# A macaron transformer layer on one core: in the last group of heads GpSimd adds the exponentials of four key tiles before the product with ones

## The chip, the cores and the metric

The kernel runs on 1 core of one Trainium2 chip. The metric is the device time of one execution in microseconds (us). Before the change it is 2382.53 us, the median of three runs (2381.05 to 2382.56).

Engines are called TensorE (PE in the rows; PEld is its weight load), VectorE (DVE), ScalarE (ACT), GpSimd (POOL) and SyncE (SP, which issues the DMAs).

## The reference

For each of 8 sequences of 1024 tokens and 512 features the layer computes a routed half step, an attention step and a second routed half step:

```
x = x + 0.5 * ffn(layernorm(x))
x = x + attention(layernorm(x))
x = x + 0.5 * ffn(layernorm(x))

ffn(x):        scores = x @ w_router
               the 3/4 of the tokens with the highest scores become gelu(x @ w_block), the others stay
attention(x):  Q = x @ Wq.T, per head times q_to_latent; latent keys and values of 64 features
               logits = q_lat . latent_k / 8, causal; attn = softmax(logits)
               heads = (attn @ latent_v) @ v_up; out = heads @ Wout.T
```

There are 16 heads of 32 features. What the change touches is the denominator of the softmax: for each query, the sum of the exponentials over all keys.

## The kernel before

**Tiles.** The 8 sequences are called batches 0 to 7 here. The 1024 tokens are 8 tiles of 128 (keys) and 2 blocks of 512 (queries). The 16 heads are 4 groups of 4 heads. All products run in float32 in three passes of high and low parts, except those with the exponentials.

**The order.** One function, `program_order`, writes a single list of events for all engines. Each engine walks that list and issues its own part of each event, in the list's order; semaphores hold it back where it needs another engine. Event names are tuples such as `("DEN", b, g, c, j)`: batch, group of heads, query block, key tile.

**Attention.** A group of heads takes 9 units (`SCORES`), called units 0 to 8 below. Units 0 to 3 are query block 1 against the full key tiles 0 to 3, 512 queries wide; units 4 to 6 are the diagonal tiles 4 to 7 of block 1 (and a piece of block 0), units 7 and 8 are block 0. In each unit:

- `S`: TensorE computes the scores of the 4 heads into 4 PSUM banks (lines 842 and 845, four passes), and ScalarE writes their exponentials into one of four slots `pr`, 128 partitions x 4 heads x 512 (line 809, four instructions).
- `AM`: GpSimd zeroes the triangle of a diagonal tile (line 715).
- `PV` and `DEN`, two units later: TensorE multiplies the exponentials by the values (line 950), and by a block of ones (line 957) to get the denominators. `PV` and `DEN` gather in one bank each over the key tiles of a query block; `LAST_TILE` says which tile is last. `HT`, `HR`, `HE` on VectorE turn, invert and multiply (lines 1116, 1119, 1121, 1127).
- A slot of `pr` is used again four units later, and ScalarE waits there for the `DEN` that read it.

**PSUM.** The units take banks from a queue of six. In the last group, `S` of units 1 to 3 waits for all four exponentials of the unit before. `S` of units 4 to 8 takes three banks of the unit before, freed by its first three exponentials, and one more: that of `SC` for unit 4, and for units 5, 6 and 7 that of the transposes `T` of unit 3, 4 and 5, which VectorE frees when it has written the low part (line 1018).

**What else runs in the last group.** In groups 0 to 2 each unit also holds products for the row maxima of the next group (`MX`, line 856) and VectorE reduces them. The last group, number 3, has none. In batches 0 to 6 it holds the first steps of the next batch instead, in this order of the list:

- `T` and `NO`, one tile per unit: ScalarE normalises (line 744), TensorE transposes (line 871), ScalarE copies the high part (line 723), VectorE subtracts it (line 1018).
- `SD`, 8 instructions in units 0 and 1: VectorE multiplies a token tile by the router's weights and sums it (line 1028, two operands from SBUF). `SM` turns four of these sums into scores (line 1035, two operands from SBUF, 4 columns). The first `SM` stands in unit 0, the second in unit 1.
- `SC`: TensorE spreads the scores over the partitions (line 877). The first `SC` stands ahead of `S` of unit 2, the second ahead of `S` of unit 3.
- `RT` for tile 0 to 7, two per unit in units 3 to 6: VectorE counts how many scores are higher (lines 1043, 1045, and 1047, which reads two operands from SBUF). In the list, `T`'s subtraction of unit 4 stands behind `RT` of tiles 0 and 1.
- `RF` and then `GX` on GpSimd (line 702, 8 instructions), in unit 7, and the first two tiles of the next batch's `F` (line 829).

In batch 7 there is no next batch. The last group holds copies of finished heads there: `HS`, a copy on ScalarE (line 723) and a subtraction on GpSimd (line 709, 128x512, two operands from SBUF).

Of the kernel before, what the change touches and what calls it, by code (L numbers as in the profile page):

```python
# [9 lines left out]
ALU = mybir.AluOpType  # L10
# [32 lines left out]

def diagonal(c, j):
    return j >= TC * c
# [12 lines left out]
ADDED = [[(1, 0)], [(1, 1)], [(1, 2)], [(1, 3)], [(1, 4)], [(1, 5), (1, 7)], [(1, 6)], [(0, 0), (0, 2)], [(0, 1), (0, 3)]]  # L58
UNITS = len(SCORES)
# [40 lines left out]
def program_order():  # L100
# [89 lines left out]
    def attention(b):  # L190
# [15 lines left out]
        def mask(n):  # L206
            g, u = units[n]
            return [("AM", b, g, c, j) for c, j in SCORES[u] if diagonal(c, j)]

        def added(n, add):  # L210
            g, u = units[n]
            return [(add, b, g, c, j) for c, j in ADDED[u]]

# [124 lines left out]
def macaron(nc, x, w_q, w_lat, w_qk, w_vu, w_out, w_router, w_block, scratch_q, scratch_o, spill_x, out):  # L338
# [47 lines left out]
    for e in sched:  # L386
# [48 lines left out]
        if k in ("PV", "DEN") and e[4] > 0:  # L435
            continue
# [6 lines left out]
    with ExitStack() as ctx:  # L443
# [14 lines left out]
        def sem(name):  # L458
            return ctx.enter_context(nc.semaphore(name))
# [16 lines left out]
        prs = [over(f"pr{n}", region[n], [P, SLOTS, HQ, BANK]) for n in range(3)]  # L476
        raw_b, raw_o, raw_q = (over(f"raw_{w}", region[0] + 8192 * n, [P, NK, E]) for n, w in enumerate("boq"))
# [54 lines left out]
        s_done, exp_ready, mask_ready = sem("s_done"), sem("exp_ready"), sem("mask_ready")  # L532
        pv_done, ac_ready, den_done, den_free = sem("pv_done"), sem("ac_ready"), sem("den_done"), sem("den_free")
# [40 lines left out]
        def pr_of(b, g, u):  # L574
            return prs[(b + 2) % 3][:, (0, 2, 1, 3)[step_nth[b, g, u] % SLOTS], :, :]

# [96 lines left out]
        def _(eng):  # L673
# [16 lines left out]
            for e in sched:  # L690
# [13 lines left out]
                elif k == "HS":  # L704
# [5 lines left out]
                                            ).then_inc(hsl_ready, 1)  # L710
                elif k == "AM":
# [7 lines left out]
        def _(eng):  # L719
# [9 lines left out]
            for e in sched:  # L729
# [68 lines left out]
                elif k == "S":  # L798
# [3 lines left out]
                    if n >= SLOTS:  # L802
                        was = steps[n - SLOTS]
                        act.wait_ge(den_done, max(nth["DEN", *was[0:2], *seg] for seg in SCORES[was[2]]))
# [14 lines left out]
        def _(eng):  # L819
# [42 lines left out]
            for e in sched:  # L862
# [90 lines left out]
                elif k == "DEN":  # L953
                    b, g, c, j = e[1:]
                    own, w = exps_of(b, g, c, j)
                    for h in range(HQ):
                        m = eng.matmul(bank(e)[h * DH:(h + 1) * DH, BANK - w:BANK], ones[:], own[:, h, :],  # L957
                                       start=(j == 0), stop=(j == LAST_TILE[c]), skip_group_check=True)
# [9 lines left out]
        def _(eng):  # L968
# [17 lines left out]
            for e in sched:  # L986
# [124 lines left out]
                elif k == "HT":  # L1111
# [4 lines left out]
                    nc.vector.transpose(rden[:], bank(("DEN", b, g, c, 0))).then_inc(den_free, 1)  # L1116
# [46 lines left out]
```

## Time and profile before

| | us |
|---|---|
| median of three runs | 2382.53 |
| the profiled execution, whole | 2386.42 |
| its span, first to last instruction | 2384.7 |
| TensorE busy | 2201.2 (92%) |
| VectorE busy | 1805.1 (76%) |
| ScalarE busy | 1176.3 (49%) |
| GpSimd busy | 404.6 (17%) |

The span is what the rows add up to; the whole execution holds 1.7 us around it. Busy time of TensorE counts overlapping instructions once. A timeline row begins with its start and its length in us, counted from the start of the span; where several instructions are merged (xN), the start is that of the first and the length that of all. The eight batches repeat every 287 to 291 us.

### The profile page before, as it was taken

How to read it: one execution, taken by the hardware profiler on the slowest of the kernel's cores; microseconds unless marked ns; L12 is line 12 of the kernel's file. 1: busy time of each engine (PE TensorE's matmuls, PEld its weight loads, DVE VectorE, ACT ScalarE, POOL GpSimd, SP SyncE). 2: the span in 40 equal slices, each digit the busy share in tenths (PEclk: the TensorE clock that was granted, in tenths of full speed). 3: DMA queues.
4: the chain of work that ended last, by engine and by line, in shares of the span. 5: the costliest groups of instructions: out<-in, count | busy, mean ns of one | idle time of the engine just before them, and what ended most of it. 6: DMA issues, size and time to landing. Idle time of an engine off the chain costs nothing.

```text
span 2384.7 us, 53143 instructions
## 1 busy us (share of the span) xinstructions
PE 2201.2 (92%) x21504; PEld 1338.9 (56%) x21504; DVE 1805.1 (76%) x5077; ACT 1176.3 (49%) x2070; POOL 404.6 (17%) x510
## 2 busy tenths in 40 slices
PE   5789999999999999999998999989998999999997
PEld 4544477445674456744566446754466544765455
DVE  7668767887669877788777886788767888678747
ACT  4245643556435564345644565345643557435552
POOL 2001111212102121021210212111111111121131
PEclk9889999999999999999999999999999999999999
DMA  3200021200302002020020201211021110212000
GB/s 137 106 2 2 2 83 60 72 2 2 106 36 72 3 19 89 37 72 3 19 89 36 73 2 40 68 54 55 2 71 36 70 40 2 71 36 72 2 2 36
DMA packets 69633, 106.42 MB, mean 45 GB/s; under 512 B 2576, under 2 KB 32784, under 8 KB 67344
## 3 DMA queue, kind: packets, MB, share of 16 engines
q1 hardware_dynamic: 69392, 103.03, 12.6%
q8 instruction: 173, 2.83, 0.5%
q14 instruction: 68, 0.56, 0.1%
HBM read 64.75 MB, written 37.75 MB: 43 GB/s over the span
## 4 chain that ended last, share of the span: by engine, by line
PE 75%; DVE 13%; ACT 6%; issue 5%; POOL 1%; DMA 0%; DVEq 0%; POOLq 0%; ACTq 0%
PE psum L829 29%; PE psum L842 17%; PE psum L950 10%; PE psum L957 9%; PE psum L845 5%; ACT pr L809 3%; DVE part L1093 3%; PE psum L871 2%; PE psum L856 2%; DVE psum L1095 2%; DVE junk L1043 1%; DVE nt_l L1018 1%; DVE junk L1028 1%; DVE junk L1045 1%; ACT nt_h L723 1%
## 5 line engine op out<-in xcount | busy, mean ns | idle before, releaser
L809 ACT ACTIVATE pr<-psum 128x512 f32<-128x512 f32 x1152 | 617.7, 597 | 537.8 <-PE psum L845 537.7
L842 PE MATMUL psum<-qk,qk 32*128 32x512 f32 (+3 forms) x4608 | 516.7, 371 | 63.6 <-DVE part L1093 26.9
L1095 DVE CUSTOM_DVE_ANT_0 psum<-psum,mask_b 128x512 f32<-128x512 f32 (+3 forms) x1024 | 473.1, 522 | 106.1 <-PE psum L856 104.7
L842 PEld LDWEIGHTS psum<-qk,qk 32*128 32x128 f32 x4608 | 318.6, 187 | 386.3 <-ACT pr L809 313.9
L856 PE MATMUL psum<-qk,qk 32*128 32x512 f32 (+3 forms) x4608 | 513.1, 371 | 20.6 <-DVE part L1093 19.1
L1093 DVE TENSOR_REDUCE part<-psum 128x1 f32<-128x512 f32 x512 | 325.4, 682 | 58.5 <-PE psum L856 56.5
L856 PEld LDWEIGHTS psum<-qk,qk 32*128 32x128 f32 x4608 | 312.0, 187 | 45.5 <-DVE part L1093 22.8
L950 PE MATMUL psum<-pr,v_sb 128*32 128x512 f32 (+3 forms) x3072 | 314.3, 504 | 1.6 <-ACT ht L723 1.6
L957 PE MATMUL psum<-pr,ones 128*32 128x512 f32 (+3 forms) x3072 | 308.8, 496 | 0.0
L715 POOL TENSOR_SCALAR_AFFINE_SELECT pr<-pr 128x512 f32<-128x512 f32 x256 | 161.6, 650 | 835.2 <-ACT pr L809 835.2
L744 ACT ACTIVATE norm<-x,nmr,rstd 128x512 f32<-128x512 f32 x192 | 153.3, 816 | 163.0 <-DVE nmr L1012 163.0
L845 PE MATMUL psum<-mrow,minus 1*128 1x512 f32 (+3 forms) x1536 | 217.4, 348 | 0.0
L829 PE MATMUL psum<-wb_h,nt_h 128*128 128x512 f32 x512 | 207.7, 406 | 3.0 <-ACT nt_act L768 3.0
L829 PE MATMUL psum<-wb_h,nt_l 128*128 128x512 f32 x512 | 200.9, 392 | 0.0
L1018 DVE TENSOR_TENSOR nt_l<-psum,nt_h 128x512 fp32r<-128x512 f32 x192 | 130.5, 684 | 93.0 <-ACT nt_h L723 92.6
L829 PE MATMUL psum<-wb_l,nt_h 128*128 128x512 f32 x512 | 200.8, 392 | 0.0
L702 POOL TENSOR_SCALAR x<-x,gain,shift 128x512 f32<-128x512 f32 x128 | 110.5, 879 | 358.3 <-DVE gain L1060 358.3
L871 PE MATMUL psum<-ident,norm 128*128 128x128 f32 x768 | 122.4, 289 | 30.7 <-ACT norm L744 22.8
L723 ACT ACTIVATE qk<-psum 128x512 fp32r<-128x512 f32 x128 | 76.2, 596 | 147.1 <-PE psum L829 146.9
L723 ACT ACTIVATE nt_h<-psum 128x512 fp32r<-128x512 f32 x192 | 115.9, 606 | 58.9 <-PE psum L871 58.8
L1095 DVE DVE_READ_ACCUMULATOR2_ANT part<- 128x1 f32 x1024 | 144.7, 141 | 0.0
L999 DVE BATCH_NORM_STATS2 stats<-x 128x6 f32<-128x512 f32 x192 | 131.9, 690 | 10.8 <-DMA x<-x_dram 6.5
(109 smaller groups left out, 3239.1 us busy)
## 6 DMA issues: line engine op xcount, KB each, us to landing
x<-x_dram SPq DMA_DIRECT2D x16, 1024.0 KB, 7.1
spill_x<-x SPq DMA_DIRECT2D x16, 1024.0 KB, 4.8
x<-spill_x SPq DMA_DIRECT2D x16, 1024.0 KB, 7.2
out_dram<-x SPq DMA_DIRECT2D x14, 1024.0 KB, 5.1
w_h<-scratch_o SPq DMA_DIRECT2D x28, 256.0 KB, 3.1
w_l<-scratch_o SPq DMA_DIRECT2D x28, 256.0 KB, 3.3
w_h<-scratch_q SPq DMA_DIRECT2D x6, 1024.0 KB, 4.9
w_l<-scratch_q SPq DMA_DIRECT2D x6, 1024.0 KB, 6.9
```

Of the source, the lines that this page charges most:

```text
L715: nc.gpsimd.affine_select(out=tri, in_=tri, compare_op=ALU.is_ge, fill=0.0, base=0, pattern=[[0, HQ], [1, P]], channel_multiplier=-1).then ...
L723: return nc.scalar.activation(dst, src, ACT.Copy)
L809: nc.scalar.activation(pr_of(b, g, u)[:, 2 * p + place, :], bank(e, place), ACT.Exp, scale=SCALE).then_inc(exp_ready, 1)
L829: m = eng.matmul(o, a_cols(lhs, k), b_cols(rhs, k), start=(k == 0 and t == 0), stop=(k == n - 1 and t == 2))
L842: eng.matmul(o, (k_h, k_h, k_l)[t][own, P * j:P * (j + 1)], (q_h, q_l, q_h)[t][own, queries], start=(t == 0 and at == 0), stop=False, skip ...
L845: m = eng.matmul(o, minus[row_at:row_at + 1, :].broadcast_to([1, P]), mrow[row_at:row_at + 1, queries], start=False, stop=True, skip_group ...
L856: m = eng.matmul(bank(e, place)[:, at:at + w], (q_h, q_h, q_l)[t][own, P * i:P * (i + 1)], (k_h, k_l, k_h)[t][own, BANK * block:BANK * blo ...
L871: m = eng.transpose(bank(e)[:, n * P:(n + 1) * P], norm[:, slot, n * P:(n + 1) * P], ident[:])
L950: m = eng.matmul(bank(e)[h * DH:(h + 1) * DH, BANK - w:BANK], v_sb[:, j, P * g + DH * h:P * g + DH * (h + 1)], own[:, h, :], start=(j == 0 ...
L957: m = eng.matmul(bank(e)[h * DH:(h + 1) * DH, BANK - w:BANK], ones[:], own[:, h, :], start=(j == 0), stop=(j == LAST_TILE[c]), skip_group_ ...
L1093: m = nc.vector.tensor_reduce(top_of, scores, AX_X, ALU.max)
L1095: m = nc.vector.tensor_tensor_reduce(scores, scores, mask_b[:, BANK - w:BANK], 1.0, FAR, ALU.add, ALU.max, top_of)
```

## The change

For query block 1 of the last group, GpSimd adds the exponentials of key tiles 0 to 3 into a buffer `acc` (event `AD`, three additions of 128x2048 elements per batch), and the product with ones runs once on that sum in place of four times. `DEN` of key tiles 0, 1 and 2 is gone in that group; `DEN` of key tile 3 reads `acc` and begins the sum. `acc` lies where the queries and keys of group 2 were. A slot of units 0 to 3 is now given back by `PV` and `AD` and no more by `DEN`.

```diff
+def first_tile(e):
+
+    return ADDENDS - 1 if e[0] == "DEN" and e[2] in SUMMED and e[3] == 1 else 0
...
+SUMMED, ADDENDS = (NQ - 1,), 4
...
         def mask(n):
             g, u = units[n]
+            if g in SUMMED and 0 < u < ADDENDS:
+                return [("AD", b, g, u)]
             return [("AM", b, g, c, j) for c, j in SCORES[u] if diagonal(c, j)]
 
         def added(n, add):
             g, u = units[n]
+            if add == "DEN" and g in SUMMED and u < ADDENDS - 1:
+                return []
             return [(add, b, g, c, j) for c, j in ADDED[u]]
...
+        accs = [[over(f"acc{n}_{m}", region[n] + 16384 * m, [P, HQ, BANK]) for m in range(2)] for n in range(3)]
...
+        def acc_of(b, g):
+
+            return accs[(b + (g - 1) // 2) % 3][(g - 1) % 2]
...
+                elif k == "AD":
+                    b, g, j = e[1:]
+                    pool.wait_ge(exp_ready, 2 * nth["S", b, g, j, 1])
+                    if j > 1:
+                        pool.wait_ge(add_ready, nth[e] - 1)
+                    acc = acc_of(b, g)
+                    nc.gpsimd.tensor_tensor(acc[:], exps_of(b, g, 1, 0)[0] if j == 1 else acc[:], exps_of(b, g, 1, j)[0], ALU.add
+                                            ).then_inc(add_ready, 1)
...
                     if n >= SLOTS:
                         was = steps[n - SLOTS]
-                        act.wait_ge(den_done, max(nth["DEN", *was[0:2], *seg] for seg in SCORES[was[2]]))
+                        if was[1] in SUMMED and was[2] < ADDENDS:
+                            act.wait_ge(pv_done, nth["PV", *was[0:2], 1, was[2]])
+                            act.wait_ge(add_ready, nth["AD", *was[0:2], max(was[2], 1)])
+                        else:
+                            act.wait_ge(den_done, max(nth["DEN", *was[0:2], *seg] for seg in SCORES[was[2]]))
...
                 elif k == "DEN":
                     b, g, c, j = e[1:]
                     own, w = exps_of(b, g, c, j)
+                    if c == 1 and g in SUMMED and j == ADDENDS - 1:
+                        own = acc_of(b, g)
+                        pe.wait_ge(add_ready, nth["AD", b, g, j])
                     for h in range(HQ):
                         m = eng.matmul(bank(e)[h * DH:(h + 1) * DH, BANK - w:BANK], ones[:], own[:, h, :],
-                                       start=(j == 0), stop=(j == LAST_TILE[c]), skip_group_check=True)
+                                       start=(j == first_tile(e)), stop=(j == LAST_TILE[c]), skip_group_check=True)
                     m.then_inc(den_done, 1)
```

What the list makes of it, on the two engines concerned. On TensorE, in the last group of batch 2, units 2 and 3 before (L842 and L845 are the scores, L950 `PV`, L871 the transposes, L957 `DEN`, L877 `SC`):

```order
L845 MATMUL psum<-mrow,minus 128x512 x4
L950 MATMUL psum<-pr_93,v_sb 32x512 x4
L871 MATMUL psum<-ident,norm 128x128 x4
L957 MATMUL psum<-pr_93,ones 32x512 x4
L877 MATMUL psum<-ident,scol 128x128 x4
L842 MATMUL psum<-qk_4_63,qk_6_65 128x512 x4
```

and now, where the same lines are numbered 874, 979, 900, 906 and 871:

```order
L874 MATMUL psum<-mrow,minus 128x512 x4
L979 MATMUL psum<-pr_93,v_sb 32x512 x4
L900 MATMUL psum<-ident,norm 128x128 x4
L906 MATMUL psum<-ident,scol 128x128 x4
L871 MATMUL psum<-qk_4_63,qk_6_65 128x512 x4
```

The `DEN` between the transposes and `SC` is gone, and likewise in units 3 and 4; in unit 5 it stands where it stood.

On GpSimd, the last two groups of batch 2 before (L715 `AM`, L702 `GX`):

```order
L715 AFFINE_SELECT pr_93<-pr_93 128x4x128 x15
L702 TENSOR_SCALAR x_49<-x_49,gain,shift 128x512 x8
L715 AFFINE_SELECT pr_93<-pr_93 128x4x128 x3
```

and now, with `AD` as line 734 and lines 715 and 702 as 740 and 719:

```order
L740 AFFINE_SELECT pr_93<-pr_93 128x4x128 x10
L734 TENSOR_TENSOR acc_0_95<-pr_93 128x2048
L734 TENSOR_TENSOR acc_0_95<-acc_0_95,pr_93 128x2048 x2
L740 AFFINE_SELECT pr_93<-pr_93 128x4x128 x5
L719 TENSOR_SCALAR x_49<-x_49,gain,shift 128x512 x8
L740 AFFINE_SELECT pr_93<-pr_93 128x4x128 x3
```

Three additions stand ahead of the group's first `AM`. In batch 7 `HS` stands between the second addition and the third:

```order
L734 TENSOR_TENSOR acc_0_99<-pr_92 128x2048
L734 TENSOR_TENSOR acc_0_99<-acc_0_99,pr_92 128x2048
L726 TENSOR_TENSOR nt_l<-ht,nt_h 128x4x128
L734 TENSOR_TENSOR acc_0_99<-acc_0_99,pr_92 128x2048
L726 TENSOR_TENSOR nt_l<-ht,nt_h 128x4x128
L740 AFFINE_SELECT pr_92<-pr_92 128x4x128
```

No instruction of VectorE or SyncE is added, removed or moved.

## Rows read from the trace of the kernel before

**Rows 1.** The page: busy time of the engines, and the chain's shares.
```profile
PE 2201.2 (92%) x21504; PEld 1338.9 (56%) x21504; DVE 1805.1 (76%) x5077; ACT 1176.3 (49%) x2070; POOL 404.6 (17%) x510
PE 75%; DVE 13%; ACT 6%; issue 5%; POOL 1%; DMA 0%; DVEq 0%; POOLq 0%; ACTq 0%
```
**Rows 2.** Groups of instructions by form: busy us, mean ns of one, idle before them.
```profile
L957 PE MATMUL psum<-pr,ones 128*32 128x512 f32 x1536 | 205.6, 607 | 0.0
...
L709 POOL TENSOR_TENSOR nt_l<-ht,nt_h 128x512 fp32r<-128x512 f32 x64 | 82.2, 1288 | 248.4 <-ACT nt_h L723 248.4
```
**Rows 3.** Timeline of TensorE, batch 3's last group, second SC and units 3 to 6.
```profile
1137.61 0.98 PE L842 MATMUL psum<-qk,qk 32*128 32x512 f32 x12
...
1141.79 0.62 PE L877 MATMUL psum<-ident,scol 128*128 128x128 f32 x4 [0.40 <-DVE scol L1035]
1142.34 0.97 PE L842 MATMUL psum<-qk,qk 32*128 32x512 f32 x12
...
1145.06 1.06 PE L957 MATMUL psum<-pr,ones 128*32 128x512 f32 x8
1146.05 0.97 PE L842 MATMUL psum<-qk,qk 32*128 32x512 f32 x12
...
1149.76 1.08 PE L842 MATMUL psum<-qk,qk 32*128 32x384 f32 x24
...
1153.63 0.98 PE L842 MATMUL psum<-qk,qk 32*128 32x256 f32 x24
```
**Rows 4.** Timeline of ScalarE, the same group: exponentials of units 1 to 3.
```profile
1134.15 2.07 ACT L809 ACTIVATE pr<-psum 128x512 f32<-128x512 f32 x4 [1.38 <-PE psum L845]
...
1138.84 2.07 ACT L809 ACTIVATE pr<-psum 128x512 f32<-128x512 f32 x4 [0.47 <-PE psum L845]
...
1143.59 2.07 ACT L809 ACTIVATE pr<-psum 128x512 f32<-128x512 f32 x4 [0.54 <-PE psum L845]
1145.51 0.63 ACT L723 ACTIVATE nt_h<-psum 128x512 fp32r<-128x512 f32 x1
1145.99 0.84 ACT L744 ACTIVATE norm<-x,nmr,rstd 128x512 f32<-128x512 f32 x1
```
**Rows 5.** Timeline of VectorE, the same group.
```profile
1135.95 0.75 DVE L1028 SCALAR_TENSOR_TENSOR junk<-x,mv,wr 128x512 bf16<-128x512 f32 x1
...
1136.74 0.16 DVE L1035 TENSOR_TENSOR scol<-dots,rstd 128x4 f32<-128x4 f32 x1
...
1141.48 0.16 DVE L1035 TENSOR_TENSOR scol<-dots,rstd 128x4 f32<-128x4 f32 x1
...
1150.13 0.68 DVE L1018 TENSOR_TENSOR nt_l<-psum,nt_h 128x512 fp32r<-128x512 f32 x1
```
**Rows 6.** Timelines of GpSimd and VectorE where both read SBUF; the last pair is a counter-case.
```profile
2.84 0.29 POOL L687 TENSOR_SCALAR_AFFINE_SELECT earlier<-earlier 128x128 bf16<-128x128 bf16 x1
...
1169.86 1.81 POOL L715 TENSOR_SCALAR_AFFINE_SELECT pr<-pr 128x512 f32<-128x512 f32 x3
...
1169.97 2.24 DVE L1066 SCALAR_TENSOR_TENSOR x<-nt_act,sel,x 128x512 f32<-128x512 f32 x1 [2.74 <-ACT nt_act L768]
...
1270.95 1.01 POOL L697 TENSOR_TENSOR rstd<-var,half 128x4 f32<-128x4 f32 x1 [12.10 <-DVE var L1007]
...
1271.38 0.74 DVE L1028 SCALAR_TENSOR_TENSOR junk<-x,mv,wr 128x512 bf16<-128x512 f32 x1
```
**Rows 7.** Stretches of batch 3's first group: TensorE's busy time, granted clock; a `PV` there.
```profile
1011.30:1014.70 3.40, 1.62 (x28) 1.02 (x24) 3.36 (x13) 2.85 (x4) 0.00 (x0) 1.00 0.00 0
1014.70:1018.10 3.40, 1.74 (x20) 1.15 (x16) 3.40 (x9) 1.08 (x2) 0.00 (x0) 0.50 0.00 0
...
1018.87 1.94 PE L950 MATMUL psum<-pr,v_sb 128*32 128x512 f32 x8
```
**Rows 8.** Batch 7's last group: exponentials of unit 1, `DEN` of key tile 3.
```profile
2289.55 2.06 ACT L809 ACTIVATE pr<-psum 128x512 f32<-128x512 f32 x4 [2.13 <-PE psum L845]
...
2302.48 1.04 PE L957 MATMUL psum<-pr,ones 128*32 128x512 f32 x8
```

More of the change, by code:

```diff
@@ L434, in macaron @@
             continue
-        if k in ("PV", "DEN") and e[4] > 0:
+        if k in ("PV", "DEN") and e[4] > first_tile(e):
             continue
@@ L532, in macaron @@
         s_done, exp_ready, mask_ready = sem("s_done"), sem("exp_ready"), sem("mask_ready")
+        add_ready = sem("add_ready")
         pv_done, ac_ready, den_done, den_free = sem("pv_done"), sem("ac_ready"), sem("den_done"), sem("den_free")
@@ L1115, in _ @@
                         dve.wait_ge(heads_ready, nth[e] - 1)
-                    nc.vector.transpose(rden[:], bank(("DEN", b, g, c, 0))).then_inc(den_free, 1)
+                    nc.vector.transpose(rden[:], bank(("DEN", b, g, c, LAST_TILE[c]))).then_inc(den_free, 1)
                 elif k == "HR":
```

## The prediction

> **What bounds the kernel now.** I read the page first. TensorE is busy 92% of the span and holds 75% of the chain that ended last; VectorE holds 13% [rows 1]. So a product taken off TensorE is worth something, unless another engine is just behind it at that place. GpSimd is busy 17%, the lowest of all, which makes it look free. Then I read the last group of heads engine by engine, in batch 3; the start of that group looks alike in batches 0 to 6. On TensorE it is a chain of short steps, and two of them wait: the second `SC` waited 0.40 for VectorE's second `SM` [rows 3]. VectorE's two `SM` start at 1136.74 and 1141.48, and `SC` starts 0.15 after the second has ended (1141.64 to 1141.79) [rows 3, 5]. ScalarE starts a unit's exponentials 1.2 after the scores start (1137.61 to 1138.84) and needs 1.92 for four of them, 0.48 for the high part behind them and about 0.7 for a normalisation [rows 3, 4]. So in this group VectorE's small router steps lie between TensorE's products, and the question is what GpSimd's additions do to VectorE.
>
> **What is removed.** Three `DEN` in each of 8 batches, 24 in all. One takes TensorE 0.99 (1145.06 to the next scores at 1146.05) [rows 3]; the group's mean of 607 ns is that of instructions that overlap in fours [rows 2]. At most 24 x 0.99 = 23.8 us go. But `DEN` of unit 2 stood ahead of the `SC` that waits for `SM`: its 0.99 buys nothing. Behind units 3 and 4 the scores need the first three exponentials of the unit before, and ScalarE's own round is 1.92 + 0.48 + 0.7 = 3.1 against the present 3.7 (1142.34 to 1146.05) [rows 3, 4]. So two rounds shrink by 0.6, and a part of the rest comes back later: S of unit 6 could stand some 1.4 earlier. Undisturbed the removal is worth 1.4 a batch, not 3.
>
> **What is added.** 24 additions of 128x2048 on GpSimd. No row has that size. The nearest has the same operation on a quarter of it: 1.29 [rows 2]. From above, four of them: 5.2. From below, the part that does not grow is taken off three times: 128x128 took 0.29 and 128x512 takes 1.81/3 = 0.60 in another operation [rows 6], so 0.19 is fixed, and 4 x 1.10 + 0.19 = 4.6. I take 4.6, since one instruction pays its fixed part once. The Trainium skill (GPSIMD Engine Reference, section Performance versus the Vector engine) states 4497 ns for this size; by it each figure below would shrink by 0.1.
>
> **Where it collides.** `CB` on VectorE, which reads two operands from SBUF, was ready at 1169.97 and ended at 1172.21, 0.54 after GpSimd's three selects ended at 1171.67; it should take 0.75, as its like in rows 5 does [rows 5, 6]. So it stood still while GpSimd ran. `SD`, `SM`, `RT`'s last instruction and `HE` are of that kind; `T`'s subtraction, with one operand in PSUM, isn't. Against this stands one pair: an `SD` at 1271.38 took its normal 0.74 beside a GpSimd instruction of 1.01 [rows 6]. That one reads only 4 columns, so it may have read them before; an addition of 2048 columns reads nearly to its end. The Trainium skill (SBUF — State Buffer, section Who interferes with whom) says that such a VectorE instruction and a GpSimd instruction that reads SBUF exclude each other, whoever is first, for the whole instruction. The rows show it for 0.6 us pieces and speak against the word "whole" in the case of 4 columns; by the rule an addition blocks for its full length, by the counter-case for its reading part.
>
> **The sum for batches 0 to 6**, in batch 3's times, each with the shift from before.
> 1. The first addition may start when unit 1's exponentials end, 1134.15 + 2.07 = 1136.22 [rows 4]. VectorE is in an `SD` until 1136.70; the first `SM` comes at 1136.74 [rows 5]. GpSimd is already waiting, so it goes first, until about 1136.65 + 4.6 = 1141.25. `SM`, `SC` and the scores of unit 2 follow: `SC` at 1141.5, scores at 1142.05 in place of 1137.61. Shift +4.4.
> 2. TensorE has stood for nearly 5 us. In the first group a stretch of 3.4 us with 1.62 busy was followed by one at a granted clock of 0.50, that is 1.2 GHz, in which a `PV` took 1.94 [rows 7], where a product of the same size takes 1.06 in the last group [rows 3]. At that level `SC` and the scores of unit 2 take 1.2 more. The exponentials of unit 2 start at 1144.5, not 1138.84, and end at 1146.6.
> 3. VectorE's second `SM` comes at most 4.74 after the first, as before [rows 5], and a little less, since the high part it had to wait for is there by now: 1145.7 to 1146.0. The second addition asks at 1146.6, too late to block it. The scores of unit 3 follow the exponentials, at 1146.75: shift +4.4.
> 4. Units 3 and 4 run at ScalarE's pace, with `DEN` gone: exponentials of unit 3 from 1148.2, scores of unit 4 at 1149.8 (+3.7), those of unit 5 at 1152.95 (+3.2). Here the removal pays 1.2.
> 5. The second addition runs from 1146.7 to 1151.3 and holds up `HE`; the third starts once `HE` is through, 1151.9 to 1156.5. `RT` of tile 0 reaches its two-operand instruction at about 1153.6 and waits until 1156.5. Behind it stands `T`'s subtraction of unit 4, which frees a bank for the scores of unit 6. It starts about 1.8 later, 1158.3, and ends at 1158.9. Before it started at 1150.13 [rows 5]. The scores of unit 6 stand at 1158.95 instead of 1153.63 [rows 3]: +5.3.
> 6. The last `AM`, `GX` and `CB` come some 3 us later relative to TensorE; TensorE has six more `F` to do before the first transposes that need them, and that work covers it; without it the 3 us would be added. Net +5.4, and 7 x 5.4 = 38.
>
> **Batch 7** has no router work, but GpSimd's queue has `HS` among the additions. The third ends 3 x 4.6 + 1.3 = 15.1 after 2291.61, at 2306.7; `DEN` of key tile 3 stood at 2302.48 [rows 8], so TensorE loses 4.2 there, less nothing, since every other unit follows `DEN` in the queue. With a spell at the low clock: 5. The `AM`s behind it are late but their `PV`s are too.
>
> Sum: +43 on the profiled execution's 2386.42 us gives 2429. That execution is 3.9 above the median of 2382.53, so I predict 2425. Edits that cost nothing: the two new waits of ScalarE on `AD` (unit 5 needs only the first addition, over by 1141.3; unit 7 the third, over by 1156.5, before even the scores of unit 6), and the bank that `DEN` opens with, free long before.
>
> **The rivals.**
> A, *no exclusion*: GpSimd and VectorE run side by side, as the counter-case allows. Then batches 0 to 6 gain 1.4 each and batch 7 still loses 5 to its queue: -10 + 5, 2377. For it: one pair in rows 6, and an addition that reads two operands in turn may leave gaps. Against: `CB` stood still over three instructions. This is the case that ends on the other side; it decides if `SM` ends within 0.5 of its old place behind the `SD`.
> B, *both `SM` blocked*: if the clock stays high, step 2's exponentials end at 1145.4 and the second addition takes the port at the end of the last `SD`, before the second `SM` (1145.7). `SC` then comes at 1150.2, and the third addition still hits `RT`. The same walk gives +7.5 a batch: 7 x 7.5 + 5 = 57, 2440. The third addition passing `HE` in step 5 costs the same.
> C, *only the first wait matters*: step 5's wait for the bank is covered. Then +3.3 a batch and 28 in all: 2410.
> That the additions don't replace the products is excluded by the order of instructions.
>
> **How the numbers follow.** Forecast 0.57, A 0.11, B 0.17, C 0.15. With 5.2 in place of 4.6 for an addition, steps 1, 3 and 5 add some 1.2 a batch, 9 in all. The range takes C with its lower edge, the forecast and B up to that term: 2403 to 2447; A is left out, with a little at either end. No change means within 0.2%, 4.8 us, about what a measurement of this kernel can tell. A falls just at that edge and is split, 0.06 faster and 0.05 same. All others are slower: 0.89.
>
> **What would show it.** Right: additions of 4.6; the first `SM` of batches 0 to 6 lasting some 4.6 instead of 0.16, and TensorE waiting over 4 us ahead of the first `SC`; seven spells at clock 0.50 behind it; the second `SM` short; one of `RT`'s two-operand instructions lasting about 3; scores of unit 6 waiting for VectorE. Wrong: all `SM` at 0.16 (A), two long ones per batch (B), or additions above 5.2 or below 4.3.

## The result, and the profile after

The changed kernel takes 2427.45 us (median of 4 runs, 2425.38 to 2431.34) against 2382.55 (4 runs) of the kernel before beside it: ratio 1.0191, 95% interval 1.0177 to 1.0205. It is slower by 45 us; the forecast was 2425.0 in a range of 2403 to 2447. The profiled execution took 2428.03, its span is 2426.0 at a mean granted clock of 0.967 (before: 2386.42, 2384.7 and 0.975).

The page of the changed kernel: busy time, and shares of the chain that ended last, as in [rows 1].

```profile
PE 2194.8 (90%) x21312; PEld 1342.7 (55%) x21312; DVE 1872.6 (77%) x5077; ACT 1175.6 (48%) x2070; POOL 521.9 (22%) x534
PE 68%; DVE 18%; ACT 7%; issue 5%; POOL 1%; DMA 0%; DVEq 0%; POOLq 0%; ACTq 0%
```

TensorE issues 192 matmuls less and is less busy, yet the span is 41 longer. What grew on the chain is VectorE, 13% to 18%, although VectorE has no instruction more. The groups of instructions of the changed kernel say which of its instructions became longer.

```profile
L1159 DVE TENSOR_TENSOR ht<-ht,rden 128x512 f32<-128x512 f32 x64 | 66.6, 1041 | 3.0 <-DVE rden L1153 0.5
L1079 DVE SCALAR_TENSOR_TENSOR junk<-srow,scol,earlier 128x128 bf16<-128x128 f32 x128 | 62.0, 484 | 0.0
L1067 DVE TENSOR_TENSOR scol<-dots,rstd 128x4 f32<-128x4 f32 x32 | 34.4, 1074 | 1.1
...
L734 POOL TENSOR_TENSOR acc<-acc,pr 128x2048 f32<-128x2048 f32 x16 | 74.8, 4676 | 38.8 <-ACT pr L838 38.1
L734 POOL TENSOR_TENSOR acc<-pr 128x2048 f32<-128x2048 f32 x8 | 37.9, 4741 | 54.3 <-ACT pr L838 54.3
```

These are `HE`, the last instruction of `RT`, and `SM`: the three kinds that read two operands from SBUF while an addition runs (L734). Their means before were 0.69, 0.37 and 0.16 us. An addition has a mean of 4.68 to 4.74 us.

Batch 3's last group on VectorE and GpSimd (start, duration, idle before it in brackets). The group begins 12.54 later than before, by the exponentials of units 0 and 1.

```profile
1148.49 0.75 DVE L1060 SCALAR_TENSOR_TENSOR junk<-x,mv,wr 128x512 bf16<-128x512 f32 x1
...
1149.29 4.33 DVE L1067 TENSOR_TENSOR scol<-dots,rstd 128x4 f32<-128x4 f32 x1
...
1157.78 0.16 DVE L1067 TENSOR_TENSOR scol<-dots,rstd 128x4 f32<-128x4 f32 x1
...
1161.04 3.10 DVE L1159 TENSOR_TENSOR ht<-ht,rden 128x512 f32<-128x512 f32 x1
1164.20 0.69 DVE L1050 TENSOR_TENSOR nt_l<-psum,nt_h 128x512 fp32r<-128x512 f32 x1
1164.81 1.27 DVE L1077 TENSOR_SCALAR_CACHE_REDUCE junk<-srow,scol 128x1024 bf16<-128x1024 f32 x1
...
1166.00 2.73 DVE L1079 SCALAR_TENSOR_TENSOR junk<-srow,scol,earlier 128x128 bf16<-128x128 f32 x1
...
1170.72 0.68 DVE L1050 TENSOR_TENSOR nt_l<-psum,nt_h 128x512 fp32r<-128x512 f32 x1
```

```profile
1148.84 4.76 POOL L734 TENSOR_TENSOR acc<-pr 128x2048 f32<-128x2048 f32 x1 [6.86 <-ACT pr L838]
1159.04 4.55 POOL L734 TENSOR_TENSOR acc<-acc,pr 128x2048 f32<-128x2048 f32 x1 [5.44 <-ACT pr L838]
1163.75 4.83 POOL L734 TENSOR_TENSOR acc<-acc,pr 128x2048 f32<-128x2048 f32 x1 [0.16 <-ACT pr L838]
```

The reader is to lay the two side by side. The first `SM` begins 0.45 after the first addition and ends at 1153.62, 0.02 after it (1153.60). `HE` ends 0.55 after the second (1163.59 to 1164.14), nearly its own 0.69. `RT`'s instruction with two operands ends 0.15 after the third (1168.58 to 1168.73). Between them, with the third addition under way, `T`'s subtraction (one operand in PSUM) takes its 0.69 and a comparison over 1024 columns with one SBUF operand its 1.27. So the number of SBUF operands decides here, not the size. (One instruction in another run does not fit; it stands in the last section.)

TensorE in the same stretch, and below it the stretch of the wait and the two behind it (columns: busy PE, PEld, DVE, ACT, POOL with their counts, then granted clock).

```profile
1153.77 1.08 PE L906 MATMUL psum<-ident,scol 128*128 128x128 f32 x4 [4.52 <-DVE scol L1067]
...
1160.37 0.98 PE L871 MATMUL psum<-qk,qk 32*128 32x512 f32 x12
...
1171.45 0.98 PE L871 MATMUL psum<-qk,qk 32*128 32x256 f32 x24 [1.04 <-DVE nt_l L1050]
```

```profile
1149.40:1153.70 4.30, 0.00 (x0) 0.00 (x0) 4.30 (x2) 1.03 (x2) 4.20 (x1) 0.95 0.00 0
1153.80:1157.20 3.40, 3.40 (x24) 2.02 (x28) 3.33 (x9) 0.90 (x2) 0.00 (x0) 0.50 0.02 5
1157.30:1160.70 3.40, 3.40 (x20) 1.84 (x16) 1.75 (x6) 2.56 (x6) 1.66 (x1) 0.59 0.00 0
```

TensorE does nothing for 4.3 us and then works at a granted clock of 0.50, 1.2 GHz. The first `SM` takes 4.33 or 4.34 and the first `SC` waits 4.52 or 4.53 in each of batches 0 to 6. **A measure for all runs:** the stretch from the exponentials of unit 1 to those of unit 8 in a last group, less the same stretch before. It says how much later the group ends than it would have, had it run as before. In batches 0 to 6 of the change it is +5.34, +5.36, +4.99, +5.65, +5.37, +5.42 and +6.27, in batch 7 +6.63, together 45.0. The exponentials of the very last unit come 42.9 late; the other 2.1 were won and lost outside these groups. No run was made on those 2 us, so their cause is not shown.

Batch 7 on TensorE and GpSimd:

```profile
2343.37 1.94 PE L989 MATMUL psum<-acc,ones 128*32 128x512 f32 x8 [4.56 <-POOL acc L734]
```

```profile
2332.70 4.83 POOL L734 TENSOR_TENSOR acc<-acc,pr 128x2048 f32<-128x2048 f32 x1
2337.49 1.27 POOL L726 TENSOR_TENSOR nt_l<-ht,nt_h 128x512 fp32r<-128x512 f32 x1
2338.73 4.49 POOL L734 TENSOR_TENSOR acc<-acc,pr 128x2048 f32<-128x2048 f32 x1
```

There the sum itself is late. The units follow each other every 3.0 us in this group and an addition takes 4.5 to 4.8, so the product waits 4.56 for the third, which stands behind an `HS` in GpSimd's queue.

### The profile page after: what moved, and what is told of

Read it like the earlier page. It is cut to its first block, busy times and chain, and to the rows that moved or that the text cites. A ratio compares the mean times of both kernels' runs of the same rounds, so it can differ in the third digit from the quotient of the medians.

```text
span 2426.0 us, 52807 instructions
## 1 busy us (share of the span) xinstructions
PE 2194.8 (90%) x21312; PEld 1342.7 (55%) x21312; DVE 1872.6 (77%) x5077; ACT 1175.6 (48%) x2070; POOL 521.9 (22%) x534
## 4 chain that ended last, share of the span: by engine, by line
PE 68%; DVE 18%; ACT 7%; issue 5%; POOL 1%; DMA 0%; DVEq 0%; POOLq 0%; ACTq 0%
PE psum L858 28%; PE psum L871 15%; PE psum L979 9%; PE psum L989 7%; PE psum L874 4%; ACT pr L838 4%; DVE part L1125 3%; DVE junk L1077 2%; PE psum L885 2%; DVE junk L1075 2%; DVE psum L1127 2%; DVE nt_l L1050 2%; DVE junk L1079 2%; PE psum L900 1%; DVE scol L1067 1%
## 5 line engine op out<-in xcount | busy, mean ns | idle before, releaser
L871 PE MATMUL psum<-qk,qk 32*128 32x512 f32 (+3 forms) x4608 | 522.7, 376 | 76.2 <-ACT pr L838 30.4
L871 PEld LDWEIGHTS psum<-qk,qk 32*128 32x128 f32 x4608 | 322.7, 190 | 393.7 <-ACT pr L838 312.2
L979 PE MATMUL psum<-pr,v_sb 128*32 128x512 f32 (+3 forms) x3072 | 320.9, 514 | 2.9 <-ACT ht L748 1.6
L989 PE MATMUL psum<-pr,ones 128*32 128x512 f32 (+3 forms) x2816 | 273.3, 485 | 0.0
L714 POOL TENSOR_TENSOR rstd<-var,half 128x4 f32<-128x4 f32 x48 | 48.6, 1012 | 510.1 <-DVE var L1039 510.0
```

The source lines that it names most:

```text
L871: eng.matmul(o, (k_h, k_h, k_l)[t][own, P * j:P * (j + 1)], (q_h, q_l, q_h)[t][own, queries], start=(t == 0 and at == 0), stop=False, skip ...
```

## The experiments

The theory to test: a two-SBUF-operand instruction of VectorE waits for the addition under way, and TensorE waits for it; the removal is worth 1.4 a batch. The rivals: the loss is the removal's or the clock's own; GpSimd's queue makes it; any work on GpSimd does. Each ratio is to runs of the kernel before that were made beside the run. "b0-6" is the mean over seven batches of the measure above, "b7" that of the last batch, both from ScalarE's timelines of the profiled execution.

| run | us | ratio to before, interval | b0-6 | b7 |
|---|---|---|---|---|
| the change | 2427.45 | 1.0191 (1.0177 to 1.0205) | +5.49 | +6.63 |
| additions_alone | 2429.04 | 1.0192 (1.0178 to 1.0206) | +5.80 | +5.55 |
| removal_alone | 2374.40 | 0.9958 (0.9945 to 0.9970) | -1.34 | -0.13 |
| split_additions | 2426.78 | 1.0187 (1.0173 to 1.0201) | +5.00 | +7.41 |
| scalar_product | 2463.18 | 1.0325 (1.0304 to 1.0346) | +8.60 | +5.95 |
| dots_early | 2399.99 | 1.0071 (1.0058 to 1.0084) | +0.24 | +7.00 |
| dots_early_before | 2380.93 | 0.9995 (0.9986 to 1.0004) | -0.84 | 0.00 |
| one_input | 2397.85 | 1.0069 (1.0051 to 1.0086) | +2.37 | -0.09 |
| groups_1_2 | 2413.97 | 1.0131 (1.0117 to 1.0144) | -0.02 | -0.01 |
| late_sum | 2440.22 | 1.0240 (1.0226 to 1.0254) | +6.71 | +6.55 |
| two_additions | 2375.00 | 0.9970 (0.9958 to 0.9981) | -1.98 | +0.73 |
| later_comparisons | 2375.96 | 0.9975 (0.9965 to 0.9986) | -2.64 | +7.61 |
| best | 2370.76 | 0.9947 (0.9933 to 0.9960) | -2.65 | 0.00 |

**additions_alone: the additions without the removal.**

```diff
...
-            if add == "DEN" and g in SUMMED and u < ADDENDS - 1:
-                return []
...
-                    if c == 1 and g in SUMMED and j == ADDENDS - 1:
-                        own = acc_of(b, g)
-                        pe.wait_ge(add_ready, nth["AD", b, g, j])
```

ScalarE waits for `DEN` and for `AD` before it uses a slot again.

> The additions run as in the change, but nobody uses their sums: TensorE does all of the DEN products as before. Theory (the additions block VectorE, the removal is worth 1.4 us a batch): the stalls of the change stay (first SM some 4.3 us in each of 7 batches, the SC of the first half waits 4.5 us), and the 8 x 1.4 = 11 us that the removal paid are lost: 2435 to 2440 us. Rival (part of the loss comes from the removal itself, by leaving TensorE without work that would keep its clock up while it waits): 2420 to 2427, since the three DEN products fall into the gaps; the DEN of unit 0 stands behind the stalled SC, so this rival is weak for the first stall.

Measured: 2429.0, within 2 us of the change. The first `SM` and the first `SC` wait as before the edit (rows of VectorE and TensorE, batch 3):

```profile
1154.13 4.33 DVE L1060 TENSOR_TENSOR scol<-dots,rstd 128x4 f32<-128x4 f32 x1
```

```profile
1158.61 1.09 PE L902 MATMUL psum<-ident,scol 128*128 128x128 f32 x4 [4.52 <-DVE scol L1060]
```

The additions cost 5.8 us a batch though nobody uses them: the loss is theirs. But the 11 us that I expected on top of 2427 did not come. In the change the removal pays 0.3 a batch (5.80 against 5.49), not 1.4. Batch 7 loses 5.55 here, although no product waits for the sum. TensorE stands for a mask there, which GpSimd has behind its additions:

```profile
2345.05 1.93 PE L975 MATMUL psum<-pr,v_sb 128*32 128x512 f32 x8 [4.16 <-POOL pr L738]
```

**removal_alone: the removal without the additions.** The mask list returns nothing in place of `AD`, and the first `DEN` reads tile 3 alone, so the denominators lack key tiles 0 to 2. The run is there for its time only.

```diff
...
-                return [("AD", b, g, u)]
+                return []
...
```

> No additions; TensorE leaves out the DEN products of the key tiles 0 to 2 in the last group, so the denominators of the second block lack these tiles there. Theory: the gain of the removal with nothing against it is 1.4 us in each of 8 batches, 2371 us (2368 to 2374), not 3 x 0.99 x 8 = 24 us (2359), because TensorE waits at SC for SM in any case. Rival (the products only fill waits): 2382, same as before. The first SM is 0.16 us again.

Measured: 0.42% faster, 8.7 us; -1.32 to -1.35 in each of batches 0 to 6. In batch 7 nearly nothing (-0.13), where the expectation had counted a full share: there the units follow each other every 3.0 us with and without `DEN`. So the removal's worth in a batch was sized right, and it is real only where nothing else holds unit 6 up. Both runs together name what does: in the change TensorE waits 1.04 before unit 6 for `T`'s subtraction behind the held `RT` (row above); what units 3 to 5 won is given back there.

**split_additions: four pieces of 128x512.**

```diff
-                    acc = acc_of(b, g)
-                    nc.gpsimd.tensor_tensor(acc[:], exps_of(b, g, 1, 0)[0] if j == 1 else acc[:], exps_of(b, g, 1, j)[0], ALU.add
-                                            ).then_inc(add_ready, 1)
+                    acc, was, own = acc_of(b, g), exps_of(b, g, 1, 0)[0], exps_of(b, g, 1, j)[0]
+                    for h in range(HQ):
+                        m = nc.gpsimd.tensor_tensor(acc[:, h, :], was[:, h, :] if j == 1 else acc[:, h, :], own[:, h, :], ALU.add)
+                    m.then_inc(add_ready, 1)
```

> Each addition of 128x2048 is issued as four of 128x512 (some 1.2 us each). Theory (a VectorE operation with two SBUF inputs waits until the GpSimd instruction under way has ended, then goes first): the first SM takes at most 1.3 us in place of 4.33, HE and the comparison with equality at most 1.9 and 1.6; the first SC waits at most 1.5 us more than before; 2427 falls to 2385 to 2400 us. Rival 1 (GpSimd keeps the port over instructions that follow at once): SM stays at 4.3 us and the time at 2427 or above, since four instructions have more fixed cost. Rival 2 (clock phases make most of the loss): 2410 to 2420.

The time was missed (2426.8 against 2385 to 2400), the mechanism held. VectorE and GpSimd in batch 3:

```profile
1152.33 1.10 DVE L1068 TENSOR_TENSOR scol<-dots,rstd 128x4 f32<-128x4 f32 x1
...
1153.95 1.24 DVE L1061 SCALAR_TENSOR_TENSOR junk<-x,mv,wr 128x512 bf16<-128x512 f32 x1
...
1155.23 1.65 DVE L1061 SCALAR_TENSOR_TENSOR junk<-x,mv,wr 128x512 bf16<-128x512 f32 x1
...
1158.60 1.62 DVE L1061 SCALAR_TENSOR_TENSOR junk<-x,mv,wr 128x512 bf16<-128x512 f32 x1
...
1160.26 1.10 DVE L1068 TENSOR_TENSOR scol<-dots,rstd 128x4 f32<-128x4 f32 x1
```

```profile
1151.88 6.12 POOL L735 TENSOR_TENSOR acc<-pr 128x512 f32<-128x512 f32 x4 [6.87 <-ACT pr L839]
1158.15 5.66 POOL L735 TENSOR_TENSOR acc<-acc,pr 128x512 f32<-128x512 f32 x4
```

VectorE does get in between two pieces: no wait is longer than one piece. But now each `SD` of the second half waits 0.4 to 0.9 too, both `SM` take 1.10, and it is the second `SC` that waits 4.60 and more, while the first waits 1.30. In the change the one long wait of `SM` had kept the `SD`s behind it clear of the addition: all 128 `SD` took 0.71 to 0.75 there. I had counted the waits that I saw, not those that they were shielding.

**scalar_product: `SM` no longer held.** Four products of one column, each with a per-partition scalar.

```diff
-                    nc.vector.tensor_tensor(scol[:, own], dots[:, own], rstd[:, 2 * f, own], ALU.mult).then_inc(scol_ready, 1)
+                    for i in range(TC * c, TC * (c + 1)):
+                        m = nc.vector.tensor_scalar(scol[:, i:i + 1], dots[:, i:i + 1], rstd[:, 2 * f, i:i + 1], None, ALU.mult)
+                    m.then_inc(scol_ready, 1)
```

> The SM of four columns, one tensor_tensor product of two SBUF tiles, is issued as four tensor_scalar products of one column each with a per-partition scalar; all else as in the change. Theory (only operations that stream two SBUF inputs are held off): the four take some 0.5 us together though the addition is under way, the first SC waits under 1 us, and what is left is the wait of HE and of the comparison with equality behind the later additions, and batch 7: 2393 us (2385 to 2402). Rival 1 (any VectorE read of SBUF after a GpSimd start waits, or SM waits for a semaphore of the addition): SM's first column takes 4.3 us, 2427. Rival 2 (HE and RT would cost as much once SM does not wait): 2415 to 2425.

The worst run of all, 1.0325. Batch 3 on VectorE, GpSimd and TensorE:

```profile
1170.32 0.58 DVE L1068 TENSOR_SCALAR scol<-dots,rstd 128x1 f32<-128x1 f32 x4
...
1171.41 3.82 DVE L1060 SCALAR_TENSOR_TENSOR junk<-x,mv,wr 128x512 bf16<-128x512 f32 x1
...
1175.27 4.86 DVE L1060 SCALAR_TENSOR_TENSOR junk<-x,mv,wr 128x512 bf16<-128x512 f32 x1
```

```profile
1169.88 4.81 POOL L734 TENSOR_TENSOR acc<-pr 128x2048 f32<-128x2048 f32 x1 [6.87 <-ACT pr L838]
1174.98 4.61 POOL L734 TENSOR_TENSOR acc<-acc,pr 128x2048 f32<-128x2048 f32 x1 [0.30 <-ACT pr L838]
```

```profile
1182.97 1.08 PE L906 MATMUL psum<-ident,scol 128*128 128x128 f32 x4 [8.59 <-DVE scol L1068]
```

`SM` passes the addition (0.58 for four), as the theory has it. It waits for the same semaphores as before, so none of them was what held it. The wait moves to the two `SD` behind it: the first is held by addition one, the second by addition two, which is ready at once because TensorE was not held up. The second `SC` then waits 8.59. This is rival B of the prediction with other victims.

**dots_early, and its control dots_early_before.** The same edit in the change and in the kernel before.

```diff
-                chunks[i // 2] += dot(0, b + 1, i)
+                groups[2][8 + i] += dot(0, b + 1, i)
```

> The change with the eight dot products of the next batch's router and their two SM moved from the first eight halves of the last group into the group before it, where GpSimd adds nothing. Theory: the 4.5 us wait of the first SC and the clock that falls after it are gone in 7 batches; HE and the first comparison with equality still wait behind the second and third addition (up to 3 us each), which delays the T subtraction of unit 4 by some 2 us, of which the removal pays 1.3: 0 to +1.5 us a batch; batch 7 keeps its 6.6: 2380 to 2400 us, 2390 likeliest. Rival (HE and the comparison are worth as much as SM): 2415 to 2427.

> The kernel before with the same move of the dot products. Theory: VectorE has the room for 6 us more in the group before the last (70% busy there), the 0.4 us wait of SC goes: 2376 to 2384 us. Rival (VectorE is short of time beside the maxima and holds TensorE up): 2390 or more; then the cost belongs to the move and is taken off the reading of dots_early.

The control is equal to before (0.9995): it loses 0.94 a batch in the third group and wins 0.84 in the last. With nothing of two operands before `SC`, the change falls from 2427 to 2400: 27 us of its 45 went with the `SM` wait and its clock. Of the 18 that are left, 7.0 is batch 7 and 6.5 is the third group, which is longer by what the control shows. In the last groups of batches 0 to 6 only step 5 of the prediction remains (VectorE, then TensorE, batch 3):

```profile
1144.24 4.51 DVE L1159 TENSOR_TENSOR ht<-ht,rden 128x512 f32<-128x512 f32 x1
...
1150.47 2.85 DVE L1079 SCALAR_TENSOR_TENSOR junk<-srow,scol,earlier 128x128 bf16<-128x128 f32 x1
```

```profile
1155.80 0.98 PE L871 MATMUL psum<-qk,qk 32*128 32x256 f32 x24 [1.42 <-DVE nt_l L1050]
```

By the exponentials of batch 3, counted from unit 1, unit 5 stands 2.85 earlier than before and unit 6 only 0.44: the held `RT` takes 2.4 back, which `HE`, held for 4.51, does not. In batches 0 and 5 a spell at the low clock follows that wait, and the group ends 1.0 late; in the other five it ends 0.05 to 0.11 early.

**one_input: GpSimd reads one operand.** It writes one tile's exponentials over `acc` in place of adding, so the denominators lack key tiles 0 to 2.

```diff
-                    acc = acc_of(b, g)
-                    nc.gpsimd.tensor_tensor(acc[:], exps_of(b, g, 1, 0)[0] if j == 1 else acc[:], exps_of(b, g, 1, j)[0], ALU.add
+                    nc.gpsimd.tensor_scalar(acc_of(b, g)[:], exps_of(b, g, 1, j)[0], 1.0, 0.0, ALU.mult, ALU.add
                                             ).then_inc(add_ready, 1)
```

> In place of each addition GpSimd writes the unit's exponentials times 1 plus 0 (tensor_scalar, one SBUF input, 128x2048), so the denominators lack the key tiles 0 to 2 in the last group. By the GX of 128x512 at 0.91 us each takes 3.6 to 3.7 us. Theory (a GpSimd instruction that streams SBUF holds VectorE's two-input reads off, whatever its own number of inputs; GX and CB stand so in the kernel before): the first SM takes 3.3 us, the time falls by about 7 x 1 for the shorter instruction: 2408 to 2422 us. Rival (only a GpSimd instruction of two inputs holds it off): SM 0.16 us, 2371 to 2380 us.

```profile
1142.96 2.15 POOL L733 TENSOR_SCALAR acc<-pr 128x2048 f32<-128x2048 f32 x1 [6.87 <-ACT pr L837]
```

```profile
1143.40 1.72 DVE L1066 TENSOR_TENSOR scol<-dots,rstd 128x4 f32<-128x4 f32 x1
```

The size was wrong: an instruction has 1.98 us in the mean, not 3.6, and the time lies below the expected range. The mechanism held: `SM` begins inside it and ends 0.01 after it (1145.11 to 1145.12). So it isn't GpSimd's number of operands that holds VectorE; a shorter instruction costs less, 16 us in all against 45. The mean of +2.37 hides a spread from +0.24 to +4.07: in batches 1, 2, 3, 5 and 6 GpSimd's second instruction comes just ahead of the second `SM`, holds it for 1.8 as well, and TensorE waits 2.64 to 2.66 for the second `SC`. In batches 0 and 4 it comes after it.

**groups_1_2: the sums in the second and third group.**

```diff
-SUMMED, ADDENDS = (NQ - 1,), 4
+SUMMED, ADDENDS = (1, 2), 4
```

> The sums are made in the second and third group of heads and not in the last. VectorE's operations there read PSUM and at most one SBUF tensor (maxima, statistics); only HE reads two. Theory: the three DEN products of 0.99 us that go in each group shorten it where TensorE is the bound (96% busy there), HE waits up to 4.3 us behind the first addition and delays the maxima queued behind it: between -2.5 and +2.5 us a group, 16 groups: 2343 to 2423 us, 2375 likeliest. Rival (the additions cost about 5 us wherever they stand, because GpSimd slows VectorE's every read of SBUF): 2445 or more.

Measured 1.0131, inside the wide expected range, but by another way. The third group takes as long as before to 0.1 us: three `DEN` gone and nothing gained; what sets that group's length was not tested. The second loses 5.2 in batch 3 (37.4 in all). VectorE and GpSimd there:

```profile
1078.52 2.32 DVE L1039 TENSOR_SCALAR var<-mv 128x4 f32<-128x4 f32 x1
...
1086.50 0.16 DVE L1044 SCALAR_TENSOR_TENSOR nmr<-mv,rstd 128x4 f32<-128x4 f32 x1 [2.29 <-POOL rstd L714]
```

```profile
1075.89 9.60 POOL L734 TENSOR_TENSOR acc<-acc,pr 128x2048 f32<-128x2048 f32 x2
1085.43 1.04 POOL L714 TENSOR_TENSOR rstd<-var,half 128x4 f32<-128x4 f32 x1
```

The statistics of the next batch pass through both engines: `VA` is held, then `RS` stands behind the additions in GpSimd's queue, then `NM` waits 2.29 for it, with the maxima behind `NM`. `HE`, which I had named, slipped through between two additions. Batch 7 has the additions too, but no next batch whose statistics could be held, and its second group loses 0.04.

**late_sum: the sum used two units later.**

```diff
-            if add == "DEN" and g in SUMMED and u < ADDENDS - 1:
+            if add == "DEN" and g in SUMMED and u < ADDENDS:
                 return []
-            return [(add, b, g, c, j) for c, j in ADDED[u]]
+            late = [(add, b, g, 1, ADDENDS - 1)] if add == "DEN" and g in SUMMED and u == ADDENDS + 1 else []
+            return [(add, b, g, c, j) for c, j in ADDED[u]] + late
...
```

> The change, but TensorE takes the product with the sum two units later (after the DEN products of unit 5) and starts the accumulation with the DEN of unit 4. Theory: in batches 0 to 6 the sum was there in time and nothing changes (+5.4 us each stays); in batch 7 the 4.56 us wait for the third addition goes, and with it most of the 6.6 us: 2427.5 - 5.5 = 2422 us (2418 to 2425). Rival (the wait moves in batch 7 to the exponentials or to HE): 2427. Rival (the early wait for the sum costs in every batch): 2410 or less.

The forecast was missed: the run is slower than the change. Batch 7 keeps +6.55; TensorE, then GpSimd:

```profile
2353.51 1.94 PE L980 MATMUL psum<-pr,v_sb 128*32 128x512 f32 x8 [4.25 <-POOL pr L741]
```

```profile
2352.83 0.62 POOL L741 TENSOR_SCALAR_AFFINE_SELECT pr<-pr 128x512 f32<-128x512 f32 x1
```

`DEN` no longer waits, and the `PV` of unit 4 does, for the mask `AM` that stands behind the same additions and two `HS`. Batch 7's price is GpSimd's queue, whoever waits for it, as additions_alone had shown; the expectation's first rival was right in kind. In the other batches the moved product makes it 1.2 a batch dearer: TensorE waits for `T` before unit 6 in any case (1.54 to 2.67 here, at most 1.42 in the change), and a product that had filled this wait stands where none is.

**two_additions.** dots_early and late_sum together, with `ADDENDS` 3.

```diff
-SUMMED, ADDENDS = (NQ - 1,), 4
+SUMMED, ADDENDS = (NQ - 1,), 3
```

> Three key tiles summed by two additions in place of four by three (ADDENDS 3), the dot products early as in dots_early, the sum used two units later. Theory: nothing two-input of VectorE that TensorE waits for meets an addition any more (HE does, with 2 us of slack behind it), so the 2.4 us that the T subtraction of unit 4 gave back in dots_early stay: about -2.2 + 0.9 = -1.3 us a batch, batch 7 within 1 us of before: 2372 us (2368 to 2378), below both kernels. Rival (HE behind the second addition holds the T subtraction of unit 3 long enough to stop TensorE): 2380 to 2390.

0.30% faster than before, 6.8 us. Without the third addition `RT` isn't held (0.35 at most), and the 2.4 us stay (-1.98 within the last group, +0.9 in the one before). The forecast of 2372 was 3 too low, in the range.

**later_comparisons.** dots_early and late_sum, three additions, and

```diff
-                chunks[6 + i] += [("RT", 0, b + 1, i)]
+                chunks[8 + i] += [("RT", 0, b + 1, i)]
...
-            chunks[14] += [("RF", 0, b + 1)]
+            chunks[16] += [("RF", 0, b + 1)]
```

> All three additions, the dot products early, the sum used two units later, and the eight comparisons RT one unit later (8 + i in place of 6 + i), so that the T subtraction of unit 4 stands ahead of the one that the third addition holds. Theory: the 2.85 us won by unit 5 stay, less 0.9 in the group before: -1.9 us a batch, batch 7 +1 to +2: 2370 us (2366 to 2378). Rival (the comparisons then end too late for GX and the next projection): what is won is lost at the first F of the next batch, 2382 or more.

-2.64 a batch, 0.7 better than two_additions: with `T`'s subtraction ahead of the held comparison the third addition costs nothing. The comparisons end in time. Batch 7 was mis-sized, +7.6 and not +1 to +2, by the queue that additions_alone and late_sum show.

**best.** later_comparisons with the last batch as before:

```diff
-            if g in SUMMED and 0 < u < ADDENDS:
+            if b + 1 < B and g in SUMMED and 0 < u < ADDENDS:
```

and the same condition wherever `SUMMED` is asked.

> later_comparisons with the last batch as in the kernel before: no additions there, all seven DEN products, since GpSimd's queue (mask and subtractions of the heads behind three additions) took 7.6 us of what the other batches won. Theory (batch 7's price is that queue alone and adds up with the rest): 2376 - 7.6 = 2368.4 us (2364 to 2372). Rival (GpSimd's queue in batch 7 is not the cause, or clock phases take it back): 2374 to 2380.

Batch 7 is at 0.00, the others keep -2.65. It is 0.53% faster than the kernel before (interval 0.40 to 0.67%) and 2.3% faster than the change; 2 above the forecast. Its batch: -2.65 + 0.95 in the group before = -1.7, seven times 12. Of the -2.65, the earlier dot products give 0.84 and the removal 1.34 in runs of their own. The move of the comparisons has no such run in the kernel before, so whether the other 0.5 is its own is not shown.

## Why the prediction was right

**What is removed.** 1.4 a batch against a measured 1.34 (removal_alone): right, also that it is not three times 0.99. For batch 7 it counted no gain, and there was none. In the change itself 0.3 of it was left.

**What is added.** 4.6 against 4.68 and 4.74, inside the bounds 4.6 to 5.2. Single additions took 4.49 to 4.84; pieces of 128x512 have a mean of 1.35 to 1.54, waits included.

**Steps 1 and 2.** In the times of before plus 12.54, `SC` was due at 1154.0 and came at 1153.77; the exponentials of unit 2 were due at 1157.0 and came at 1156.90; the clock fell to 0.50. The shift there is +5.5, forecast +5.7. In additions_alone the shift is there by the exponentials of unit 3 and stays the same up to unit 8 (+5.9 in batch 3), so these two steps, with the rest of their low spell, are the whole price of the additions in batches 0 to 6. dots_early shows that it goes with them.

**Step 3.** The second `SM` was free (0.16) in all seven batches; it ended 0.7 to 1.1 before the second addition began. But in batch 3 the scores of unit 3 came at 1160.37, +5.5 and not +4.4: `PV` and the products around it were at the low clock too (granted 0.50 and 0.59 in the stretches above), and I had ended the spell with the scores of unit 2. Step 4 inherits this: units 4 and 5 at +4.7 and +4.2, forecast +3.7 and +3.2. Batches 0, 4 and 5 are like batch 3. In batches 1, 2 and 6 the clock was back sooner, as the same two stretches of batch 6 show:

```profile
2033.70:2037.10 3.40, 3.40 (x24) 1.72 (x28) 3.33 (x9) 1.20 (x3) 0.00 (x0) 0.53 0.00 0
2037.30:2040.70 3.40, 3.40 (x40) 1.71 (x32) 2.90 (x7) 3.40 (x8) 2.06 (x1) 0.99 0.00 0
```

There the exponentials of units 3, 4 and 5 stood at +4.2, +3.6 and +2.9, close to the forecast.

**Step 5** made good for it, since it does not hang on step 4: its clock is the chain of additions. `RT`'s instruction was due to end at 1169.0 and ended at 1168.73, `T`'s subtraction was due at 1170.8 and began at 1170.72, the scores of unit 6 at +5.3 as forecast. So the error of 1.1 in steps 3 and 4 was absorbed there, which was luck. What I had not said clearly is that this step only takes back the removal's gain; alone (dots_early) it costs 2.4. In every batch `HE` ended some 0.55 after the second addition, and the third addition followed at once. Batch 6 came to +6.27 because the clock fell a second time behind TensorE's wait before unit 6: those scores took 1.53 there, in place of 0.98.

**Step 6** held as far as the times show: outside the last groups nothing was lost in sum, 2 us came back.

**Batch 7** is the mis-sized term, 5 forecast and 6.63 measured. The chain of additions took 15.25 (2327.97 to 2343.22), forecast 15.1, and the wait was 4.56, forecast 4.2. The rest is the low clock: the `DEN` took 1.94, in place of 1.04 [rows 8], and the scores behind it 1.65, in place of 0.98. "Less nothing, since every other unit follows" passed over a second wait of nearly the same length, that for the mask behind the same additions: it stops TensorE for 4.16 in additions_alone, where no product waits for the sum.

**The sum.** 5.4 x 7 + 5 = 43 on the profile, measured 41.6 (2428.03 less 2386.42): 45.0 inside the last groups, less what came back outside them. The mean of +5.49 stands for batches from +4.99 to +6.27, so its nearness to 5.4 is in part chance. **The rivals.** A fell (all first `SM` 4.33). B did not occur in the change, but one_input has it in five batches, and scalar_product made it by letting TensorE run on. C fell: +5.49, not +3.3.

The pairs above settle for long instructions what the counter-case in [rows 6] had left in doubt. The Trainium skill (SBUF — State Buffer, section Who interferes with whom) has the lock for the whole instruction; for additions of 2048 columns, for pieces of 512 and for a one-operand copy the traces agree (`SM` ended 0.02, 0.02 and 0.01 after the GpSimd instruction). In the counter-case of 4 columns they do not: it occurs seven times in the kernel before, and the `SD` took 0.74 each time. The case for the wait was also stronger than the one `CB` that I showed: 11 of 64 began inside an instruction of GpSimd before, with a mean of 1.78, and the others have 0.74.

## What to carry to other kernels

- An engine that is 17% busy is not free if a busier engine's instructions have to wait while its own run. Before work goes to GpSimd, list VectorE's instructions with two SBUF operands in that stretch and who waits behind each; then the instructions behind them, which the first wait may be shielding: in split_additions, scalar_product and late_sum a wait only moved.
- Move the short instructions that others wait for out of the stretch first (here 8 dot products and two `SM`, free in themselves), and put what must be on time ahead of what may be held. Then 21 of the 24 additions, which together had cost 1.9%, stood in a kernel 0.5% faster than before.
- If a late sum is the wait, look at the whole queue that makes it late before its use is moved: late_sum only changed who waits.

## What the runs showed of the hardware that was not expected

- A `TENSOR_SCALAR` of 4 columns with one SBUF operand (`var` from `mv`) took 2.32 us beside an addition in seven of 48 cases of groups_1_2, where it took 0.17 in all 48 cases of the kernel before. Products of one column by the same instruction (0.58 for four) and comparisons with a sum over 1024 columns (1.27) were not held. "Two SBUF operands" is thus not the whole condition. The Trainium skill (SBUF — State Buffer, the same section) adds VectorE's two-port modes to it, which would fit; no run here separates them.
- GpSimd's copy with a multiply and an add of constants took 1.98 us for 128x2048, while its `GX` with two per-partition scalars takes 0.76 at the least for 128x512 and 0.92 in the mean: four of those would be 3.0 to 3.7.
- GpSimd lets VectorE in between two of its instructions, even when the next is ready: no wait in split_additions exceeded one piece.
